# Heads in cycles of three steps, with the sums of own and of cross keys copied out of PSUM in two parts

## The chip, the cores and the metric

The kernel runs on one core of one Trainium2 chip. The metric is the device time of one execution in microseconds (us): the median of the runs shown. The profile is of one such execution.

## What is computed

One decoder layer with the norms after each part, for 8 sequences of 512 rows with 256 channels, and a context of 1024 rows with 128 channels each:

```python
x = layernorm(x + linear_attention(x))       # 16 heads of 64, relu features
x = layernorm(x + xattn(x, ctx))             # the part that the change touches
x = layernorm(x + top1_moe(x))               # 8 experts, 256 -> 1024 -> 256

# xattn: 16 heads of 16 channels
att  = causal(q @ k.T * scale)               # 512 x 512: own keys
y    = softmax(att) @ v
attc = qc @ kc.T * scale                     # 512 x 1024: cross keys
y    = y + softmax(attc) @ vc
out  = y @ Wp + bp
```

Each softmax has a sum of its own, so a head needs two sets of weighted values, one over own keys and one over cross keys, and each is divided by its own denominator.

## The kernel before

A loop over the 8 sequences (batches) computes both attentions and the routing, and after it a loop over tiles of rows runs the experts. The change is in the stretch of each batch that treats the 16 heads of the second attention, two at a time: 8 pairs (`PAIRS`). Head `a` of a pair lies in 64 of the 128 partitions, so the matmuls of the two heads use the two halves of TensorE's rows and can run side by side when they alternate.

The work of a pair is of these kinds. The names are those of the list `ORDER`, which every engine walks through in the same order and takes its own part of:

- **max** (22 for each pair, `MAXES`): TensorE computes scores of queries by keys for one head (L773 for cross keys, one matmul of 512 columns; L770 for own keys), into one of three PSUM banks, and VectorE reduces the bank to the row maxima (L1412; L1408 for own keys, with the causal mask). The banks are a ring of `MBANKS = 3`: an entry of the ring waits in `ring_slot` until the entry three places earlier has been read.
- **row**: when all maxima of a pair are there (VectorE's small `mpad` operation, L1419), TensorE turns them around (L781) into a bank of the same ring, and ScalarE copies them to `mrow` (L1193, four copies).
- **exp** (11 steps for each pair, `NU`: 3 for own keys, 8 for cross keys): TensorE computes the scores again, keys by queries, for both heads, and subtracts the maxima with a second matmul (L807 and L809 for cross keys, L800 and L803 for own keys). ScalarE takes the exponential (L1201) from PSUM into one of four buffers in SBUF (`ERING = 4`). There are two PSUM places for the scores, so the scores of step k wait until the exponential of step k-2 is through: `pe.wait_ge(s_exp, cur(b, NEXP, k - 1))`. The exponential of step k waits until step k-4 has been weighed. For own keys, GpSimd cuts the upper triangle off (L661).
- **weigh** (11 for each pair): TensorE multiplies values by exponentials (L837) and sums them in one PSUM bank, `zbank`: its left half for own keys, its right half for cross keys. Four such matmuls use four groups of 32 columns of the array at once. Each stands as 8 records of 256 columns where a step is of cross keys.
- **keep**: ScalarE copies `zbank` to `zk` (L1210). **turn**: TensorE turns `zk` around (L848) into a bank of the ring, ScalarE copies it out (L1218), VectorE takes the reciprocals (L1425), and GpSimd does the divisions and the addition.
- **part**: pieces of other matmuls (the query features of the next batch, L857), at the start and at the end of the stretch.

`heads_order` writes the list by hand. In the steady part it goes on by two steps at a time. With m for a max and E for an exp, one block is

```
[turn]  weigh weigh  m  E  m m  E  m
```

where the weighs are those of four and three steps before (`BEHIND = 4`). A row stands 4 or 6 maxima behind the last max of its pair (`ROW_AFTER`), in practice at the end of a block. If the last weigh of a pair has just been issued, and its keep with it, the first weigh of the next pair is put off to the end of the block (`late`), because it writes the bank that the keep reads. The maxima run ahead of the exps, so the last 15 steps of a batch have no max beside them.

On the way in, the maxima of the first pair and some of the second are mixed with `FIRST_PARTS`. On SyncE's queue, `free_slot` waits until a pair's last scores are computed before it loads the keys and queries of the pair five places on into its place.

Of the kernel before, what the change touches and what calls it, by code (L numbers as in the profile page):

```python
# [33 lines left out]
E, HID = 8, 1024  # L34
# [46 lines left out]
HB = 2  # L81
PAIRS = XH // HB
# [12 lines left out]
NSELF = len(EXP_SELF)  # L95
NU = NSELF + NTC
# [3 lines left out]
MAXES = NMU * HB  # L100
ERING = 4
AHEAD = 8
ROW_AFTER = (4, 6)
BEHIND = 4
LATER = 2

# [4 lines left out]
def head_half(j, a):  # L111
# [5 lines left out]
FIRST_PARTS = [("v", 1, 3), ("qc1", 0, 3), ("q1", 0, 3), ("k1", 0, 3),  # L117
               ("qf0", 0, 4), ("qf0", 1, 4), ("qf1", 0, 4), ("qf1", 1, 4)]
# [3 lines left out]
def heads_order():  # L122


    maxima = []
    for p in range(PAIRS):
        maxima += [("max", p, m) for m in range(MAXES)]
    for p in range(PAIRS):
        at = maxima.index(("max", p, MAXES - 1)) + 1 + (ROW_AFTER[p % 2] if p + 1 < PAIRS else 0)
        maxima.insert(at, ("row", p, 0))  # L130

    def take(count):
        taken = []
        while maxima and (count or maxima[0][0] == "row"):
            count -= maxima[0][0] == "max"
            taken.append(maxima.pop(0))
        return taken

    order = []
    for name, part, count in FIRST_PARTS:  # L140
        order += take(count)
        order.append(("part", name, part))
    order += take(MAXES + AHEAD - sum(count for _, _, count in FIRST_PARTS))
    turns, late = [], []
    steps = PAIRS * NU
    for k in range(0, steps + BEHIND, 2):
        weighed = late + [m for m in (k - BEHIND, k - BEHIND + 1) if m >= 0]
        late = []
        if turns:
            order.append(turns.pop())  # L150
        for m in weighed:
            if m % NU == 0 and m and order[-1] == ("keep", m // NU - 1, 0):
                late.append(m)
                continue
            order.append(("weigh", *divmod(m, NU)))
            if m % NU == NU - 1:
                order.append(("keep", m // NU, 0))
                turns.append(("turn", m // NU, 0))
        order += take(1)
        if k < steps:  # L160
            order.append(("exp", *divmod(k, NU)))
        order += take(HB)
        if k + 1 < steps:
            order.append(("exp", *divmod(k + 1, NU)))
        order += take(1)
        order += [("weigh", *divmod(m, NU)) for m in late]
        late = []
    assert not maxima
    return order + [("part", "qf2", 0)] + turns + [("part", "qf2", 1)]


ORDER = heads_order()


# [17 lines left out]
NEXP = PAIRS * NU  # L192


TILE = 128
TH = TILE // P
NTILE = (B * T + E * (TILE - 1)) // TILE
assert NTILE % 2 == 1
MORE = T // TILE
CR = C + 1  # L200
E_STEPS = 30
NOBODY = float(1 << 20)
# [28 lines left out]
def attentions(nc, x, xT, ctxT, wqkT, wv_l, rf, w_out, b_out, wk, bk, wq, bq, wv, bv, wck, bck,  # L231
# [9 lines left out]
    with ctx:  # L241
        def sb(name, shape, dt=F32):
            return ctx.enter_context(nc.sbuf_tensor(name, shape, dt))
# [84 lines left out]
        zk = sb("zk", [P, 2, T // 2])  # L328
# [12 lines left out]
        iota = sb("iota", [P, B * NT])  # L341
        number = sb("number", [P, B * NT])
        upto = sb("upto", [P, NTILE])
        full_at = sb("full_at", [P, MORE])
        below = sb("below", [P, E + 1, E])
        ranked = sb("ranked", [P, (NT + 1) * E])
        place = sb("place", [P, E])
        room = sb("room", [P, E])
        over = sb("over", [P, E])
        more = sb("more", [P, E, MORE])  # L350
        fresh = sb("fresh", [P, E])
        prior = sb("prior", [P, E + 1, E])
        first = sb("first", [P, E + 1])
# [14 lines left out]
        zbank = ps[1][:, BANK:2 * BANK]  # L368
# [33 lines left out]
        s_av = sem("s_av")  # L402
# [4 lines left out]
        s_keep = sem("s_keep")  # L407
# [15 lines left out]
        def cur(b, per, k):  # L423

            return b * per + (per + k)
# [269 lines left out]
        def _(pe):  # L695
# [116 lines left out]
            def weigh(b, p, n):  # L812


                if p == 0 and n == 0:
                    pe.wait_ge(s_vone, b + 1)
                if n == 0:
                    pe.wait_ge(s_keep, cur(b, PAIRS, p))
                e, own = es[:, (p * NU + n) % ERING], n < NSELF
                if own:  # L820
                    pe.wait_ge(s_cut, cur(b, PAIRS * NSELF, p * NSELF + n + 1))
                else:
                    pe.wait_ge(s_exp, cur(b, NEXP, p * NU + n + 1))
                z = zbank[:, 0:T // 2] if own else zbank[:, T // 2:T]
                for j, col in (EXP_SELF[n] if own else [(n - NSELF, 0)]):
                    first = j if own else 0
                    for f in range(2):
                        tiles = [t for t in (f, f + 2) if t >= first]
                        if not tiles:
                            continue  # L830
                        for a in range(HB):
                            at = a * BANK + col + (tiles[0] - first) * P
                            weights = e[:, at:at + P] if len(tiles) == 1 else \
                                e[:, a * BANK + col:a * BANK + col + T].rearrange("p (c f t) -> p c f t", c=2, f=2)[:, :, f, :] \
                                if first == 0 else e[:, at:at + 3 * P].rearrange("p (c t) -> p c t", c=3)[:, 0:3:2, :]
                            row = (f * HB + a) * ZW
                            last = mm(z[row:row + VW, (2 - len(tiles)) * P:2 * P], (va if own else vca)[:, j, p * HB + a, :], weights,  # L837
                                      start=n in (0, NSELF), stop=n in (NSELF - 1, NU - 1))
                last.then_inc(s_av, 1)

            def turn_results(b, p):

                pb = ring_slot(b, ("turn", p, 0))
                pe.wait_ge(s_keep, cur(b, PAIRS, p + 1))
                for w in range(2):
                    for c in range(2):
                        col = (w * 2 + c) * P
                        last = tr(pb[:, col:col + P], zk[:, w, c * P:(c + 1) * P], ident[:])  # L848
                last.then_inc(s_ring, 1)
# [37 lines left out]
            with pe.Fori(0, nb) as b:  # L887
# [17 lines left out]
                t = ready(b, "g0")  # L905
# [11 lines left out]
                t = ready(b, "g1")  # L917
# [197 lines left out]
        def _(act):  # L1115
            act.sem_inc(s_mrow, PAIRS)
            act.sem_inc(s_exp, NEXP)
            act.sem_inc(s_keep, PAIRS)
            act.sem_inc(s_zt, PAIRS - 1)

            def relu_q(i, t):
# [10 lines left out]
            with act.Fori(0, nb) as b:  # L1132
# [69 lines left out]
                                         eslot[k % 2][:].rearrange("p (a c) -> p a c", a=HB)[:, :, 0:w],  # L1202
                                         ACT.Exp, scale=SCALE).then_inc(s_exp, 1)

                def keep(p):

                    act.wait_ge(s_av, cur(b, NEXP, (p + 1) * NU))
                    if p:
                        act.wait_ge(s_ring, cur(b, NRING, RING_AT["turn", p - 1, 0] + 1))
                    nc.scalar.activation(zk[:].rearrange("p w t -> p (w t)"), zbank, ACT.Copy).then_inc(s_keep, 1)  # L1210

                def turned(p):

# [6 lines left out]
                for kind, p, n in ORDER:  # L1220
                    if kind == "row":
                        maxima_rows(p)
                    elif kind == "turn" and p < PAIRS - 1:
                        turned(p)
                    elif kind == "exp":
                        exp_unit(p, n)
                    elif kind == "keep":
                        keep(p)
                    elif p == "v":
                        values()  # L1230
                    elif p == "qc1":
                        act.wait_ge(s_nearc, (b + 1) * NEARC)
                        whole_part("qc1", 3)
                    elif p == "q1":
                        act.wait_ge(s_near, (b + 1) * NEAR)
                        whole_part("q1", 2)
                    elif p == "k1":
                        whole_part("k1", 0)
                    elif kind == "part" and n == 1:
                        relu_q(int(p[-1]), full(p)).then_inc(s_act, 1)  # L1240
# [14 lines left out]
        def _(dve):  # L1255
# [37 lines left out]
            v.tensor_copy(tri[:], y_s[:, 0, 0:P])  # L1293
            v.tensor_copy(upto[:, 0:B * NT], iota[:])
            v.tensor_scalar(upto[:, B * NT:NTILE], iota[:, 0:NTILE - B * NT], float(B * NT), None, ALU.add)
            v.tensor_scalar(full_at[:], iota[:, 0:MORE], float(TILE), None, ALU.mult)
            v.tensor_tensor(below[:], iota[:, 0:E + 1].unsqueeze(2).broadcast_to([P, E + 1, E]),
                            iota[:, 0:E].unsqueeze(1).broadcast_to([P, E + 1, E]), ALU.is_gt)
            v.reduce_sum(minus_f[:], ident[:].rearrange("p (b c) -> p c b", c=MROW)[:, 0:2, :], AX.X)
# [24 lines left out]
            with dve.Fori(0, nb) as b:  # L1324
                def step(ins):

                    steps[0] += 1
                    ins.then_inc(s_dstep, 1)
                    dve.wait_ge(s_dstep, b * NSTEP + steps[0])
# [141 lines left out]
                def by_tile(of):  # L1471
                    return of[:].unsqueeze(1).broadcast_to([P, NT, E])

                step(v.tensor_tensor(over[:], total, room[:], ALU.subtract))
                step(v.tensor_tensor(more[:], over[:].unsqueeze(2).broadcast_to([P, E, MORE]),
                                     full_at[:].unsqueeze(1).broadcast_to([P, E, MORE]), ALU.is_gt))
                step(v.reduce_sum(fresh[:], more[:], AX.X))
                step(v.tensor_tensor(prior[:], below[:], fresh[:].unsqueeze(1).broadcast_to([P, E + 1, E]), ALU.mult))
                step(v.reduce_sum(first[:], prior[:], AX.X))
# [346 lines left out]
```

## Time and profile before

| | |
|---|---|
| Median of 3 runs | 2287.46 us (2287.35 to 2288.9) |
| The profiled execution | 2287.69 us, of which the span from first to last instruction is 2286.0 us |
| TensorE busy | 2169.5 us (95%) |
| VectorE busy | 1366.7 us (60%) |
| ScalarE busy | 1102.2 us (48%) |
| GpSimd busy | 367.5 us (16%) |
| Mean granted TensorE clock | 0.994 of full speed |

Busy is the time in which at least one instruction of the engine was running. Matmuls are pipelined and their ends are modelled, so TensorE reads as busy in much of the time in which it does not start anything. Starts are more telling: the time from the start of one group of matmuls to the start of the next is what the group cost. In a line of the timeline, xN is the number of instructions of one kind that were merged, and the second number is the time from the start of the first to the end of the last. The time in brackets is how long the engine sat idle before, and who released it.

### The profile page before, as it was taken

To read this page: it belongs to the slowest core of one execution; us is meant where nothing else is said; L and a number is where in the kernel's file an instruction comes from. 1 tells how busy PE (TensorE), PEld (TensorE's weight loads), DVE (VectorE), ACT (ScalarE), POOL (GpSimd) and SP (SyncE) were. 2 spreads that over 40 slices of the span, in tenths; PEclk is the share of its full clock that TensorE was granted. 3 is DMA by queue.
4 is the path that set the end of the run, shared out by engine and by line. 5 is a ranking of instruction groups with operands and counts; after the bars stand their busy time and mean duration, and the time that the engine had idled before them with its cause. 6 is when DMAs were issued, how large, how long until landed. Compare 5 with 4: busy or idle time off the path is not lost. (4 is left out here: it accounts for less than half of the span.)

```text
span 2286.0 us, 51067 instructions
## 1 busy us (share of the span) xinstructions
PE 2169.5 (95%) x16290; PEld 1352.2 (59%) x16291; DVE 1366.7 (60%) x3905; ACT 1102.2 (48%) x1680; POOL 367.5 (16%) x628
## 2 busy tenths in 40 slices
PE   8999999999899999999999999999999899799998
PEld 4555554556455555555555645554555455499997
DVE  2588357844785458635883478357844685255554
ACT  1267524761477227732674257524762377233332
POOL 1011111111111111111111111111111111122222
PEclk9999999999999999999999999999999999899999
DMA  7440025102520162005300350026102520655553
GB/s 235 155 164 25 2 106 200 48 2 85 198 71 2 47 234 73 2 11 189 130 25 9 141 180 25 1 97 209 48 2 85 198 71 2 221 181 182 183 182 109
DMA packets 115763, 235.75 MB, mean 103 GB/s; under 512 B 19614, under 2 KB 42655, under 8 KB 113344
## 3 DMA queue, kind: packets, MB, share of 16 engines
q1 hardware_dynamic: 112112, 224.23, 29.3%
q0 software_dynamic: 3408, 8.41, 1.0%
q8 instruction: 137, 2.24, 0.4%
q14 instruction: 106, 0.87, 0.1%
HBM read 154.04 MB, written 73.17 MB: 99 GB/s over the span
## 5 line engine op out<-in xcount | busy, mean ns | idle before, releaser
L1201 ACT ACTIVATE es<-ps 128x1024 f32<-128x1024 f32 (+1 forms) x704 | 665.3, 984 | 250.7 <-PE ps L809 181.4
L1412 DVE TENSOR_REDUCE craw<-ps 128x1 f32<-128x512 f32 x1024 | 636.7, 684 | 115.0 <-PE ps L773 115.0
L773 PE MATMUL ps<-hk,hq 64*128 64x512 f32 x1024 | 391.4, 450 | 24.7 <-DVE craw L1412 8.6
L807 PE MATMUL ps<-hq,hk 64*128 64x512 f32 x1024 | 325.0, 440 | 2.2 <-ACT es L1201 2.2
L1408 DVE CUSTOM_DVE_ANT_0 ps<-ps,causal 128x512 f32<-128x512 f32 (+3 forms) x512 | 236.2, 518 | 91.4 <-PE ps L770 91.0
L773 PEld LDWEIGHTS ps<-hk,hq 64*128 64x128 f32 x1024 | 174.7, 184 | 194.8 <-DVE craw L1412 129.3
L809 PE MATMUL ps<-mrow,minus 64*128 64x512 f32 x1024 | 285.8, 391 | 0.0
L837 PE MATMUL ps<-es,vca 128*17 128x256 f32 x4096 | 276.6, 382 | 1.2 <-ACT es L1201 0.3
L661 POOL TENSOR_SCALAR_AFFINE_SELECT es<-es 128x256 f32<-128x256 f32 x256 | 99.0, 406 | 659.5 <-ACT es L1201 659.4
L1731 ACT ACTIVATE hT<-ph,b1s 128x128 f32<-128x128 f32 x312 | 89.2, 369 | 182.8 <-PE ph L1694 182.8
L809 PEld LDWEIGHTS ps<-mrow,minus 64*128 64x128 f32 x1024 | 166.0, 186 | 10.1
L807 PEld LDWEIGHTS ps<-hq,hk 64*128 64x128 f32 x1024 | 141.4, 184 | 32.0 <-ACT es L1201 20.8
L837 PEld LDWEIGHTS ps<-es,vca 128*17 128x17 f32 x4096 | 93.9, 97 | 109.9 <-issue 39.1
L770 PE MATMUL ps<-hk,hq 64*128 64x512 f32 (+3 forms) x512 | 142.8, 351 | 6.7 <-DVE craw L1408 6.2
L1694 PEld LDWEIGHTS ph<-xinT,w1s 128*128 128x128 f32 x1248 | 147.2, 194 | 3.0 <-issue 1.1
L1694 PE MATMUL ph<-xinT,w1s 128*128 128x128 f32 x1248 | 147.6, 277 | 0.7 <-ACT xinT L1721 0.7
L857 PE MATMUL ps<-xT_s,wqf 128*128 128x512 f32 x288 | 138.5, 607 | 5.0 <-ACT whole L1178 3.3
L1707 PE MATMUL py<-w2s,hT 128*128 x624 | 141.2, 380 | 0.0
L867 PE MATMUL ps<-wkf,xT_s 128*128 128x512 f32 x288 | 130.4, 597 | 0.0
L800 PE MATMUL ps<-hq,hk 64*128 64x512 f32 (+3 forms) x512 | 125.0, 337 | 4.3 <-ACT big_a L1122 4.3
L770 PEld LDWEIGHTS ps<-hk,hq 64*128 64x128 f32 x512 | 82.8, 184 | 74.7 <-DVE craw L1408 32.0
L1707 PEld LDWEIGHTS py<-w2s,hT 128*128 128x128 f32 x624 | 115.7, 190 | 13.9
(210 smaller groups left out, 2838.3 us busy)
## 6 DMA issues: line engine op xcount, KB each, us to landing
w1s<-in_w1T SPq DMA_DIRECT2D x39, 1024.0 KB, 5.4
hk<-scr_kc SPq DMA_DIRECT2D x64, 512.0 KB, 5.1
scr_kc<-staged SPq DMA_DIRECT2D x16, 1024.0 KB, 4.3
scr_qc<-staged SPq DMA_DIRECT2D x32, 512.0 KB, 4.5
scr_q<-staged SPq DMA_DIRECT2D x32, 512.0 KB, 5.3
hq<-scr_qc SPq DMA_DIRECT2D x56, 256.0 KB, 4.4
hq<-scr_q SPq DMA_DIRECT2D x56, 256.0 KB, 4.2
hk<-scr_k SPq DMA_DIRECT2D x56, 256.0 KB, 4.6
```

The lines of the kernel that those rows point to most:

```text
L770: last = mm(pb[:, col:col + w], hq[i][at, t * P:(t + 1) * P], hk[i][at, 0:w], start=True, stop=True)
L773: last = mm(pb, hq[i][at, T + t * P:T + (t + 1) * P], hk[i][at, T + half * BANK:T + (half + 1) * BANK], start=True, stop=True)
L807: mm(pb[a], hk[i][rows[a], T + j * P:T + (j + 1) * P], hq[i][rows[a], T:2 * T], start=True, stop=False)
L809: last = mm(pb[a], neg[a], mrow[p % 2][rows[a], :], start=False, stop=True)
L837: last = mm(z[row:row + VW, (2 - len(tiles)) * P:2 * P], (va if own else vca)[:, j, p * HB + a, :], weights, start=n in (0, NSELF), stop=n ...
L857: last = mm(t[:, a * T:(a + 1) * T], wqf[:, c, j * P:(j + 1) * P], xT_s[:, c, :], start=c == 0, stop=c == KC - 1)
L867: last = mm(t[:, half * 512:(half + 1) * 512], xT_s[:, c, i * P:(i + 1) * P], wkf[:, c, half * 512:(half + 1) * 512], start=c == 0, stop=c ...
L1201: nc.scalar.activation(es[:, k % ERING, :].rearrange("p (a c) -> p a c", a=HB)[:, :, 0:w], eslot[k % 2][:].rearrange("p (a c) -> p a c", a ...
L1408: last = v.tensor_tensor_reduce(own, own, causal[:, (NT - 1 - t) * P:NT * P], 1.0, LOWEST, ALU.add, ALU.max, craw[p % 2][:, t, a:a + 1, 0])
L1412: last = v.reduce_max(craw[p % 2][:, t, a:a + 1, 1 + half], pb, AX.X)
L1694: last = mm(ph[g % 2][:, a * TILE:(a + 1) * TILE], w1s[i][:, k, (GROUP * c + a) * P:(GROUP * c + a + 1) * P], xinT[i][:, k, :], start=k == ...
L1707: last = mm(py[i][:, n, 0:C], hT[i][:, c, n * P:(n + 1) * P], w2s[:, bass.ds(e * (NHC * C) + c * C, C)], start=c == 0, stop=c == NHC - 1)
```

## The change

`heads_order` is written anew. In the steady part it goes on by three steps at a time (`CYCLE = 3`). One cycle is

```
[turn]  weigh weigh weigh  [keep]  m  E  m m  E  m m  E  m  [row]
```

with the weighs of steps k-4, k-3 and k-2 ahead of the exps of steps k, k+1 and k+2. A batch has 31 such cycles where it had 46 blocks (the last two of each list with less in them). The first two cycles have two maxima more at their end (`MORE = 2`, `MORE_CYCLES = 2`), so the maxima end earlier: beside step 5 of the seventh pair, and not beside step 6. A row stands where a cycle ends. A turn stands at the start of the cycle after the one whose weighs end a pair.

A keep is now two: the left half of `zbank` is copied after the pair's third weigh, the right half after its eleventh, both at the end of the weighs of their cycle. No weigh is put off any more. TensorE waits for `s_keep` where a keep stands between a weigh and the one before it. The old constant `MORE` of the routing is renamed `MORE_TILES`. The core of the diff:

```diff
-ROW_AFTER = (4, 6)
+ROW_AFTER = 4
+MORE, MORE_CYCLES = 2, 2
+CYCLE = 3
...
+    def row_if_due(behind):
+
+        p = rows[0] if rows else None
+        if rows and (PAIRS - p - 1) * MAXES - behind >= len(maxima):
+            order.append(("row", rows.pop(0), 0))
...
     steps = PAIRS * NU
-    for k in range(0, steps + BEHIND, 2):
-        weighed = late + [m for m in (k - BEHIND, k - BEHIND + 1) if m >= 0]
-        late = []
+    for k in range(0, steps + BEHIND, CYCLE):
         if turns:
             order.append(turns.pop())
-        for m in weighed:
-            if m % NU == 0 and m and order[-1] == ("keep", m // NU - 1, 0):
-                late.append(m)
-                continue
+        for m in range(max(0, k - BEHIND), min(steps, k - BEHIND + CYCLE)):
             order.append(("weigh", *divmod(m, NU)))
-            if m % NU == NU - 1:
-                order.append(("keep", m // NU, 0))
+            if m % NU == NSELF - 1:
+                kept.append(("keep", m // NU, 0))
+            elif m % NU == NU - 1:
+                kept.append(("keep", m // NU, 1))
                 turns.append(("turn", m // NU, 0))
-        order += take(1)
-        if k < steps:
-            order.append(("exp", *divmod(k, NU)))
-        order += take(HB)
-        if k + 1 < steps:
-            order.append(("exp", *divmod(k + 1, NU)))
-        order += take(1)
-        order += [("weigh", *divmod(m, NU)) for m in late]
-        late = []
+        order.extend(kept)
+        kept = []
+        take(1)
+        for n in range(k, min(steps, k + CYCLE)):
+            order.append(("exp", *divmod(n, NU)))
+            take(HB if n + 1 < k + CYCLE else 1 + (MORE if k < MORE_CYCLES * CYCLE else 0))
+        row_if_due(min(ROW_AFTER, len(maxima)) if maxima else 0)
...
-                if n == 0:
-                    pe.wait_ge(s_keep, cur(b, PAIRS, p))
+                if n == 0 or KEPT_AT[p, n] > KEPT_AT[p, n - 1]:
+                    pe.wait_ge(s_keep, cur(b, 2 * PAIRS, KEPT_AT[p, n]))
...
-                def keep(p):
-
-                    act.wait_ge(s_av, cur(b, NEXP, (p + 1) * NU))
-                    if p:
+                def keep(p, w):
+
+                    act.wait_ge(s_av, cur(b, NEXP, KEEP_AFTER[p, w]))
+                    if p and w == 0:
                         act.wait_ge(s_ring, cur(b, NRING, RING_AT["turn", p - 1, 0] + 1))
-                    nc.scalar.activation(zk[:].rearrange("p w t -> p (w t)"), zbank, ACT.Copy).then_inc(s_keep, 1)
+                    nc.scalar.activation(zk[:, w, :], zbank[:, w * (T // 2):(w + 1) * (T // 2)], ACT.Copy).then_inc(s_keep, 1)
```

## Rows read from the trace of the kernel before

**Rows 1.** The page's first line.
```profile
span 2286.0 us, 51067 instructions
```

**Rows 2.** Busy time of each engine from a batch's opening to the end of its heads.
```profile
1092.52:1222.79 130.27, 125.83 (x1319) 73.16 (x1318) 93.51 (x232) 97.11 (x131) 19.93 (x46) 1.00 0.14 48
```

**Rows 3.** Line L1210 in the whole span: minimum, median, maximum in ns, first and last.
```profile
L1210 ACT ACTIVATE zk<-ps x64: 597/603/606, 149.7 to 1945.4; 128x512 f32<-128x512 f32 x64
```

**Rows 4.** Timeline of PE in the steady part, start and length in us.
```profile
1137.95 0.49 PE L773 MATMUL ps<-hk,hq 64*128 64x512 f32 x1
...
1139.22 0.50 PE L773 MATMUL ps<-hk,hq 64*128 64x512 f32 x1
1139.90 0.32 PE L781 MATMUL ps<-ident,mpad 128*128 128x128 f32 x1 [0.17 <-DVE craw L1412]
1140.15 1.06 PE L837 MATMUL ps<-es,vca 128*17 128x256 f32 x16
...
1142.94 1.06 PE L837 MATMUL ps<-es,vca 128*17 128x256 f32 x16
...
1145.63 0.41 PE L837 MATMUL ps<-es,vca 128*17 128x256 f32 x4
```

**Rows 5.** Timeline of DVE in the same stretch.
```profile
1138.48 2.48 DVE L1412 TENSOR_REDUCE craw<-ps 128x1 f32<-128x512 f32 x4 [0.28 <-PE ps L773]
```

**Rows 6.** Timeline of ACT in the same stretch.
```profile
1138.94 1.94 ACT L1201 ACTIVATE es<-ps 128x1024 f32<-128x1024 f32 x2 [0.95 <-PE ps L809]
```

**Rows 7.** Timeline of PE at a batch's opening, before its first weigh.
```profile
1095.71 0.49 PE L800 MATMUL ps<-hq,hk 64*128 64x256 f32 x2
...
1096.19 1.09 PE L773 MATMUL ps<-hk,hq 64*128 64x512 f32 x2
1096.87 0.64 PE L807 MATMUL ps<-hq,hk 64*128 64x512 f32 x2
...
1097.44 0.44 PE L773 MATMUL ps<-hk,hq 64*128 64x512 f32 x1
1097.81 1.28 PE L837 MATMUL ps<-es,va 128*17 128x256 f32 x20
```

**Rows 8.** Timeline of DVE in the opening and just after it.
```profile
1093.05 6.07 DVE L1412 TENSOR_REDUCE craw<-ps 128x1 f32<-128x512 f32 x10 [1.64 <-PE ps L773]
...
1102.88 0.46 DVE L1408 CUSTOM_DVE_ANT_0 ps<-ps,causal 128x256 f32<-128x256 f32 x1
...
1103.63 1.29 DVE L1412 TENSOR_REDUCE craw<-ps 128x1 f32<-128x512 f32 x2
```

**Rows 9.** Timeline of ACT in the opening.
```profile
1094.63 2.43 ACT L1201 ACTIVATE es<-ps 128x1024 f32<-128x1024 f32 x3 [0.98 <-PE ps L803]
1097.86 1.02 ACT L1201 ACTIVATE es<-ps 128x1024 f32<-128x1024 f32 x1 [0.80 <-PE ps L809]
```

**Rows 10.** Line L1425 among the groups of two pairs, busy us and mean ns.
```profile
L1425 DVE RECIPROCAL rec<-zt 128x16 f32<-128x16 f32 x4 | 1.0, 249 | 0.0
```

**Rows 11.** Timeline of PE where no maxima are left.
```profile
1203.78 0.50 PE L807 MATMUL ps<-hq,hk 64*128 64x512 f32 x2
...
1204.45 1.06 PE L837 MATMUL ps<-es,vca 128*17 128x256 f32 x16
1205.44 0.50 PE L807 MATMUL ps<-hq,hk 64*128 64x512 f32 x2
...
1206.67 1.06 PE L837 MATMUL ps<-es,vca 128*17 128x256 f32 x16
...
1212.90 0.63 PE L837 MATMUL ps<-es,va 128*17 128x256 f32 x8
1213.46 0.66 PE L848 MATMUL ps<-ident,zk 128*128 128x128 f32 x4
1214.05 1.06 PE L837 MATMUL ps<-es,va 128*17 128x128 f32 x20
```

**Rows 12.** Timeline of ACT in the same stretch.
```profile
1206.22 1.94 ACT L1201 ACTIVATE es<-ps 128x1024 f32<-128x1024 f32 x2 [0.27 <-PE ps L809]
```

More of the change, by code:

```diff
@@ L122, in heads_order @@
 def heads_order():
[L125 to L130, printed above, removed]
-    def take(count):
[L133 to L137, printed above, removed]
@@ L139, in heads_order @@
-    order = []
+    maxima = [("max", p, m) for p in range(PAIRS) for m in range(MAXES)]
+    order, rows, turns, kept = [], list(range(PAIRS)), [], []
+    def take(count):
+        order.extend(maxima[:count])
+        del maxima[:count]
+    def row_if_due(behind):
+        p = rows[0] if rows else None
+        if rows and (PAIRS - p - 1) * MAXES - behind >= len(maxima):
+            order.append(("row", rows.pop(0), 0))
     for name, part, count in FIRST_PARTS:
-        order += take(count)
+        take(count)
+        row_if_due(ROW_AFTER)
@@ L142, in heads_order @@
         order.append(("part", name, part))
-    order += take(MAXES + AHEAD - sum(count for _, _, count in FIRST_PARTS))
-    turns, late = [], []
+    take(MAXES + AHEAD - sum(count for _, _, count in FIRST_PARTS))
     steps = PAIRS * NU
-    for k in range(0, steps + BEHIND, 2):
-        weighed = late + [m for m in (k - BEHIND, k - BEHIND + 1) if m >= 0]
-        late = []
+    for k in range(0, steps + BEHIND, CYCLE):
         if turns:
             order.append(turns.pop())
-        for m in weighed:
-            if m % NU == 0 and m and order[-1] == ("keep", m // NU - 1, 0):
-                late.append(m)
-                continue
+        for m in range(max(0, k - BEHIND), min(steps, k - BEHIND + CYCLE)):
@@ L192 @@
 NEXP = PAIRS * NU
+KEPT_AT = {(p, n): sum(f[0] == "keep" for f in ORDER[:i]) for i, (kind, p, n) in enumerate(ORDER) if kind == "weigh"}
+KEEP_AFTER = {(p, n): sum(f[0] == "weigh" for f in ORDER[:i]) for i, (kind, p, n) in enumerate(ORDER) if kind == "keep"}
 TILE = 128
@@ L198 @@
 assert NTILE % 2 == 1
-MORE = T // TILE
+MORE_TILES = T // TILE
 CR = C + 1
@@ L343, in attentions @@
         upto = sb("upto", [P, NTILE])
-        full_at = sb("full_at", [P, MORE])
+        full_at = sb("full_at", [P, MORE_TILES])
         below = sb("below", [P, E + 1, E])
@@ L349, in attentions @@
         over = sb("over", [P, E])
-        more = sb("more", [P, E, MORE])
+        more = sb("more", [P, E, MORE_TILES])
         fresh = sb("fresh", [P, E])
@@ L843, in turn_results @@
                 pb = ring_slot(b, ("turn", p, 0))
-                pe.wait_ge(s_keep, cur(b, PAIRS, p + 1))
+                pe.wait_ge(s_keep, cur(b, 2 * PAIRS, 2 * p + 2))
                 for w in range(2):
@@ L1117, in _ @@
             act.sem_inc(s_exp, NEXP)
-            act.sem_inc(s_keep, PAIRS)
+            act.sem_inc(s_keep, 2 * PAIRS)
             act.sem_inc(s_zt, PAIRS - 1)
@@ L1227, in _ @@
                     elif kind == "keep":
-                        keep(p)
+                        keep(p, n)
                     elif p == "v":
@@ L1295, in _ @@
             v.tensor_scalar(upto[:, B * NT:NTILE], iota[:, 0:NTILE - B * NT], float(B * NT), None, ALU.add)
-            v.tensor_scalar(full_at[:], iota[:, 0:MORE], float(TILE), None, ALU.mult)
+            v.tensor_scalar(full_at[:], iota[:, 0:MORE_TILES], float(TILE), None, ALU.mult)
             v.tensor_tensor(below[:], iota[:, 0:E + 1].unsqueeze(2).broadcast_to([P, E + 1, E]),
@@ L1474, in _ @@
                 step(v.tensor_tensor(over[:], total, room[:], ALU.subtract))
-                step(v.tensor_tensor(more[:], over[:].unsqueeze(2).broadcast_to([P, E, MORE]),
-                                     full_at[:].unsqueeze(1).broadcast_to([P, E, MORE]), ALU.is_gt))
+                step(v.tensor_tensor(more[:], over[:].unsqueeze(2).broadcast_to([P, E, MORE_TILES]),
+                                     full_at[:].unsqueeze(1).broadcast_to([P, E, MORE_TILES]), ALU.is_gt))
                 step(v.reduce_sum(fresh[:], more[:], AX.X))
```

## The prediction

> **What bounds the kernel now.** I read the page first, for the span [rows 1], then the busy time of each engine over the heads of one batch [rows 2]. The reader is to see that no engine alone explains the 130.27 us: TensorE reads as busy for 125.83, but its matmuls are pipelined, VectorE works 93.51 and ScalarE 97.11. The heads are 8 times 130.27 = 1042 us, 46% of the span: of the 64 keeps, 8 in a batch, the first stands at 149.7 and the last at 1945.4 [rows 3], which is 7 periods of about 241 us and one batch's own stretch between. The experts behind them are untouched.
>
> Then I read timelines of starts, to find what paces a block. Four rules come out, and the rest is made of them.
>
> *VectorE's beat.* Ten reductions in a row take 6.07 us, start to end, so one starts every 0.60 [rows 8], and four take 2.48 [rows 5]; I use 0.61. Six are 3.66.
>
> *The ring gate.* A max's matmul starts at 1137.95 and its reduction at 1138.48: 0.53 later. The fourth max of that block starts at 1139.22, which is 0.74 after the start of the reduction (0.68 long) that frees its bank. The row waits for the second reduction, which started 0.61 behind the first, at 1139.09, and starts at 1139.90: 0.81 [rows 4, 5].
>
> *ScalarE's gate.* In the opening, the exponential of the first step starts at 1094.63 [rows 9]. One takes 1.02 [rows 9], so it ends at 1095.65, and the scores of the third step start at 1095.71 [rows 7]: 0.06 later. In a block, the exponential starts 0.99 behind the block's first matmul (1137.95 to 1138.94 [rows 4, 6]).
>
> *Phases of TensorE.* A group of two weighs of cross keys holds TensorE from 1204.45 to 1205.44, 0.99, and a single one from 1212.90 to 1213.46, 0.56 [rows 11]. So a weigh adds 0.43, and three take 1.42. A whole block that nothing holds up takes 1145.63 - 1142.94 = 2.69 [rows 4]: 0.99 of weighs and 1.70 of scores. In it the fourth max may start 0.53 + 0.74 = 1.27 behind the first by the ring gate, just when it comes up in the order anyway. The block of two steps is as long as three banks allow, and VectorE needs 2.44 of its 2.69.
>
> **The change, part by part.**
>
> *Fewer and longer groups of weighs.* In a batch they go from 47 to 30. Without gates a cycle would cost TensorE 1.42 of weighs and 18 matmuls of scores instead of 12. Three more pairs of them, one pair every 0.23 (two steps of eight matmuls hold 1205.44 to 1206.67, 1.23, one step 1203.78 to 1204.45, 0.67 [rows 11], the difference with one new start in it being 0.56 for two pairs; inside a step a pair follows in 0.23), bring 1.70 to 2.38. That is 3.80 for three steps where three are now 1.5 x 2.69 = 4.04.
>
> *The ring gate in a cycle.* A cycle has six maxima between two groups of weighs. The banks are still three, so the sixth needs the third reduction: it can't start before 0.53 + 2 x 0.61 + 0.74 = 2.49 behind the first. The fifth can't before 1.88, and the third step's scores stand behind it.
>
> *ScalarE's gate in a cycle.* The third step's scores use the place of the first step's: 0.99 + 1.02 + 0.06 = 2.07. From their start to the weighs it takes what the opening shows for the same order (scores, one max, weighs): 1096.87 to 1097.81, 0.94 [rows 7]. So the weighs start at 3.01, and the cycle is 1.42 + 3.00 = 4.42 us. By the ring gate alone it is 2.49 + 0.37 (1097.44 to 1097.81) + 1.42 = 4.28. I take 4.42, since both gates hold. Three steps cost 0.4 us more than three free ones of before. VectorE shows why: during the weighs it has the last three banks and no more, 1.8 us of work, then it stands still for over 0.5 until the next max arrives. Ten cycles of a batch are of this plain kind: 44.2.
>
> *Rows.* A row behind the sixth max needs the bank of the fourth: the reduction of that starts at 0.53 + 3 x 0.61 = 2.36, and the row can start 0.81 later, 3.17, and holds TensorE 0.25 (1139.90 to 1140.15 [rows 4]): 1.42 + 3.42 = 4.84. Where the reciprocal, 0.25 [rows 10], comes first on VectorE, as in most of them, it is 5.1. With one of them behind a shorter group of weighs (the own keys' third step) six such cycles are 29.9.
>
> *Turns.* A turn stands behind a cycle's last max and before its weighs, so it needs the bank of two reductions before: 3.12, and 0.59 for itself (1213.46 to 1214.05 [rows 11]): 5.1 with plain maxima. Where the own keys' maxima are ahead of it, VectorE is slower (from the last own reduction to the next one 0.75 with the `mpad` operation, 1102.88 to 1103.63 [rows 8], where plain ones follow in 0.61), and the weigh of the second step must wait for two cuts. I get 5.5 and 5.9 for those, 27.2 for the five.
>
> *The opening* is 5.29 up to the first weigh (1092.52 [rows 2] to 1097.81 [rows 7]), at VectorE's beat, and stays. The cycle after it has eight maxima, 5.4, and the last one with maxima holds a row and a turn behind the `mpad`, 6.3.
>
> *The tail.* It has 16 steps after these and no maxima, so only ScalarE's gate counts. The exponential starts 0.78 behind the scores (1205.44 to 1206.22 [rows 11, 12]), the third step's scores at 0.78 + 1.02 + 0.06 = 1.86, the weighs 0.67 on, at 2.53: a cycle of 3.95. Now two steps take 1206.67 - 1204.45 = 2.22 [rows 11], three 3.33. Five cycles of 3.95 less 0.2 for a shorter first group, one turn (0.6) and 3.8 for the last exponentials and weighs come to 24.0.
>
> *Keeps.* Eight more copies a batch. Two halves cost between 0.60 (the whole, [rows 3]) and 1.20 (each as long as it), so 0 to 0.6 more for a pair; I take nothing, because ScalarE works 97 of 130 us and the copies fall between the start of the scores and the exponential 0.99 behind it. Without that cover a batch would pay up to 5 us. The new waits on `s_keep` come a whole cycle behind the copy. Queued behind them are the weighs and then the maxima, but they don't bite. The weigh that was put off no longer is: a start of a group, 0.13 each, is in the counts.
>
> *Queues.* SyncE's `free_slot` waits for scores of a pair five places back, and its loads are used about two pairs later; no DMA is added or gets into the way. GpSimd has the same work.
>
> **The sum** for a batch: 5.29 + 5.4 + 44.2 + 29.9 + 27.2 + 6.3 + 24.0 = 142.3 us, against 130.27 now [rows 2]: +12.0. For eight batches +96. The profiled execution took 2287.69 for a span of 2286.0 [rows 1], 0.2 above the median. So 2383 us.
>
> One rule of the Trainium skill speaks for the change. *TensorEngine Tiling (Array Packing)*, Key Properties, says that going from one tiling mode to another drains TensorE, and scores (64-row tiles) and weighs (32-column tiles) are two modes. By that, the trace agrees: the last max of the opening starts 0.37 before the weighs [rows 7], where pairs within a mode follow in 0.23. [...] The same page's PSUM Bottleneck says that tiling doesn't speed up what empties PSUM, and this is the side on which I forecast.
>
> **The rivals.**
>
> *TensorE decides* (0.08). The gates are softer than I read them, and only the borders count: 3.80 for 4.04, 0.24 x 29 = 7 us a batch, 2232. It needs a reduction of 0.35 us or less, since the sixth max would have to start at 1.96 = 0.53 + 2d + 0.74. Against it: 0.61, and the opening, where ten maxima in a row run at just that beat.
>
> *It evens out* (0.04). Blocks of now aren't all free: 46 of them and the turns take 130, and 1.5 free blocks would do for less. If these hold-ups were gone in longer cycles, a change within 0.2% is possible.
>
> *Borders absorb rows and turns* (0.16). They cost now on top of free blocks; in a cycle held up anyway they might hide, and the tail might keep its present pace. Then 11 cycles cost 4.5 and not 5.2, and the tail 4 us less: about +4 a batch, 2320.
>
> *More than that* (0.04). Own reductions and `mpad` hold cycles up that I counted as plain; 0.4 for each pair would be +26, 2409.
>
> **How the numbers follow.** My forecast has 0.68: 2383, own range 2345 to 2400. The lower end is all plain cycles at 4.28, turns and rows at their shortest and half the tail's loss, +58. The upper end is the part of `mpad` left out. The 8-in-10 range reaches down into the absorbed case and a little into the last one: 2318 to 2403. About 0.2% (5 us) is what a measurement can tell from nothing. Faster 0.08, same 0.04, slower 0.88.
>
> **What would show it.** The heads of a batch take about 142 us, with 30 groups of weighs, 24 records and 1.42 us each. In a plain cycle the reductions come in one run of six, 3.66 long, with VectorE idle for 0.5 to 0.7 before the first. The sixth max starts 2.5 to 2.7 behind the first. In the waits, TensorE's for L1412 goes up, and a wait for ScalarE's L1201 appears on L807. In the tail, the weighs start every 3.95 us. It is wrong if weighs follow each other in 3.8, or if the third step's scores start before the first exponential ends.

## The result and the profile after

The changed kernel takes 2379.68 us (median of 4 runs, 2379.22 to 2382.45), the kernel before 2287.4 (4 runs): a ratio of 1.0407, 95% interval 1.039 to 1.0423. The forecast was 2383 us.

The page of the changed kernel begins like this (busy us, share of the span, instructions):

```profile
span 2377.6 us, 51267 instructions
## 1 busy us (share of the span) xinstructions
PE 2211.1 (93%) x16290; PEld 1388.5 (58%) x16291; DVE 1366.4 (57%) x3905; ACT 1113.2 (47%) x1744; POOL 366.4 (15%) x628
```

VectorE and ScalarE do what they did, within 1%, in 91.6 us more. So it is waiting. The busy time of each engine over one batch, from the first max behind `qf1` to the end of the heads, answers to [rows 2]:

```profile
1137.34:1279.12 141.78, 131.14 (x1319) 77.59 (x1318) 93.51 (x232) 98.71 (x139) 19.86 (x46) 1.00 0.13 44
```

141.78 us against 130.27 is 11.5 more for a batch and 92 for eight: all of the difference lies here. VectorE's 93.51 us are the same to the last digit.

A plain cycle is where one is to look. TensorE's timeline, from its first max at 1188.58 to the next cycle's at 1192.97, answers to [rows 4]:

```profile
1188.58 0.50 PE L772 MATMUL ps<-hk,hq 64*128 64x512 f32 x1
...
1189.86 1.09 PE L772 MATMUL ps<-hk,hq 64*128 64x512 f32 x2
1190.65 0.54 PE L806 MATMUL ps<-hq,hk 64*128 64x512 f32 x2
1190.99 0.43 PE L808 MATMUL ps<-mrow,minus 64*128 64x512 f32 x2
1191.22 0.39 PE L772 MATMUL ps<-hk,hq 64*128 64x512 f32 x1
1191.55 1.49 PE L836 MATMUL ps<-es,vca 128*17 128x256 f32 x24
1192.97 0.50 PE L772 MATMUL ps<-hk,hq 64*128 64x512 f32 x1
```

VectorE's timeline of the same stretch, which answers to [rows 5]:

```profile
1185.55 2.42 DVE L1411 TENSOR_REDUCE craw<-ps 128x1 f32<-128x512 f32 x4
1189.11 3.68 DVE L1411 TENSOR_REDUCE craw<-ps 128x1 f32<-128x512 f32 x6 [1.15 <-PE ps L772]
1193.51 2.48 DVE L1411 TENSOR_REDUCE craw<-ps 128x1 f32<-128x512 f32 x4 [0.71 <-PE ps L772]
```

And ScalarE's, which answers to [rows 6]:

```profile
1189.57 2.91 ACT L1200 ACTIVATE es<-ps 128x1024 f32<-128x1024 f32 x3 [0.99 <-PE ps L808]
```

The cycle takes 4.39 us. Its six reductions are one run of 3.68, and then VectorE stands for 0.71 until the next cycle's first max. The third step's scores start at 1190.65, 2.07 into the cycle: the first exponential ends at 1189.57 + 1.02 = 1190.59. The pair of maxima at 1189.86 stretches over 1.09 us because the second of them waited for its bank; it started 1.09 less its own 0.50 behind 1189.86, at about 1190.45. The weighs of three steps take 1.42 (1191.55 to 1192.97).

The list of waits (us in total, times, longest) shows where TensorE and its weight loads (PEld) waited. For ScalarE's exponentials they waited longer: the second of these lines was 20.8 in the kernel before and the third 2.2. The first, the wait for VectorE's reductions of cross keys, was 129.3 then and hardly moved, so it says nothing for or against the ring gate:

```profile
PEld ps L772 <- DVE craw L1411: 126.6, 272, 1.0
...
PEld ps L806 <- ACT es L1200: 49.8, 80, 1.1
...
PE ps L806 <- ACT es L1200: 22.3, 32, 0.8
```

Where no maxima are left, TensorE's timeline answers to [rows 11]:

```profile
1271.37 1.49 PE L836 MATMUL ps<-es,vca 128*17 128x256 f32 x24
1272.79 0.50 PE L806 MATMUL ps<-hq,hk 64*128 64x512 f32 x2
...
1274.63 0.50 PE L806 MATMUL ps<-hq,hk 64*128 64x512 f32 x2 [0.66 <-ACT es L1200]
...
1275.29 1.49 PE L836 MATMUL ps<-es,vca 128*17 128x256 f32 x24
```

The weighs start every 3.92 us, and in a plain cycle TensorE stands for about 0.66 until the first exponential is through. The blocks of two steps took 2.22.

### The profile page after: what moved, and what is told of

It is laid out like the page before. It is cut to its first block and busy times, and to the rows that moved or that the text cites. A ratio compares the mean times of both kernels' runs of the same rounds, so it can differ in the third digit from the quotient of the medians.

```text
span 2377.6 us, 51267 instructions
## 1 busy us (share of the span) xinstructions
PE 2211.1 (93%) x16290; PEld 1388.5 (58%) x16291; DVE 1366.4 (57%) x3905; ACT 1113.2 (47%) x1744; POOL 366.4 (15%) x628
## 5 line engine op out<-in xcount | busy, mean ns | idle before, releaser
L1200 ACT ACTIVATE es<-ps 128x1024 f32<-128x1024 f32 (+1 forms) x704 | 657.6, 984 | 227.0 <-PE ps L808 179.8
L772 PE MATMUL ps<-hk,hq 64*128 64x512 f32 x1024 | 405.5, 453 | 36.2 <-DVE craw L1407 10.2
L806 PE MATMUL ps<-hq,hk 64*128 64x512 f32 x1024 | 304.0, 440 | 23.4 <-ACT es L1200 22.3
L836 PE MATMUL ps<-es,vca 128*17 128x256 f32 x4096 | 270.0, 382 | 4.5 <-ACT es L1200 4.5
L808 PE MATMUL ps<-mrow,minus 64*128 64x512 f32 x1024 | 266.7, 391 | 0.0
L806 PEld LDWEIGHTS ps<-hq,hk 64*128 64x128 f32 x1024 | 135.1, 184 | 60.0 <-ACT es L1200 49.8
L836 PEld LDWEIGHTS ps<-es,vca 128*17 128x17 f32 x4096 | 104.5, 97 | 109.9 <-ACT es L1200 27.0
L808 PEld LDWEIGHTS ps<-mrow,minus 64*128 64x128 f32 x1024 | 149.0, 186 | 10.7
L856 PE MATMUL ps<-xT_s,wqf 128*128 128x512 f32 x288 | 137.7, 605 | 4.8 <-ACT whole L1177 3.2
L799 PE MATMUL ps<-hq,hk 64*128 64x512 f32 (+3 forms) x512 | 118.2, 338 | 9.4 <-ACT es L1200 5.2
```

What stands on the lines that cost most here:

```text
L772: last = mm(pb, hq[i][at, T + t * P:T + (t + 1) * P], hk[i][at, T + half * BANK:T + (half + 1) * BANK], start=True, stop=True)
L806: mm(pb[a], hk[i][rows[a], T + j * P:T + (j + 1) * P], hq[i][rows[a], T:2 * T], start=True, stop=False)
L808: last = mm(pb[a], neg[a], mrow[p % 2][rows[a], :], start=False, stop=True)
L856: last = mm(t[:, a * T:(a + 1) * T], wqf[:, c, j * P:(j + 1) * P], xT_s[:, c, :], start=c == 0, stop=c == KC - 1)
L1200: nc.scalar.activation(es[:, k % ERING, :].rearrange("p (a c) -> p a c", a=HB)[:, :, 0:w], eslot[k % 2][:].rearrange("p (a c) -> p a c", a ...
```

## The experiments

Twelve kernels ran on the chip; their ratios are to the kernel before, timed beside them. Six of them leave out part of the maxima or of the exponentials, only to shorten VectorE's or ScalarE's work.

**The change without its longer cycle** (called c2 below).

```diff
-MORE, MORE_CYCLES = 2, 2
-CYCLE = 3
+MORE, MORE_CYCLES = 0, 2
+CYCLE = 2
```

> The changed kernel with CYCLE = 2 and MORE = 0, so blocks of two steps, four maxima and two weighs as before, but still two keeps for each pair, the waits on the halves and no weigh put off. Theory (the length of the cycle costs, through the ring of three banks and the two places for scores): the heads of a batch are back at about 130 us and the time at 2283 to 2290 us. Rival (the keeps in two parts and the waits on them cost): the time stays above 2320 us.

Measured: 2277.69 us, ratio 0.9957 (0.9943 to 0.9971), a little below the range. The length of the cycle and the extra maxima are the whole loss: 2379.7 - 2277.7 = 102 us, more than the change lost in all. What is left of the change (two keeps, rows at a block's end, no weigh put off) gains 10 us. The steady part is as long as before (104.2 us from the first weigh to the last max, it was 104.1); the tail is 19.35 us and was 20.54. In the kernel before, the last pair's row doesn't stand at the end of a block but between the scores of steps 6 and 7 of the seventh pair, just ahead of [rows 11]; it waited 1.29 us for VectorE's `mpad` with nothing else to do:

```profile
1203.53 0.33 PE L781 MATMUL ps<-ident,mpad 128*128 128x128 f32 x1 [1.29 <-DVE mpad L1419]
```

In this kernel the row stands at the block's end and waited less:

```profile
1196.32 0.40 PE L806 MATMUL ps<-hq,hk 64*128 64x512 f32 x2
1196.55 0.40 PE L808 MATMUL ps<-mrow,minus 64*128 64x512 f32 x2
1197.79 0.33 PE L780 MATMUL ps<-ident,mpad 128*128 128x128 f32 x1 [0.84 <-DVE mpad L1418]
1198.05 1.06 PE L836 MATMUL ps<-es,vca 128*17 128x256 f32 x16
```

The block with that row takes 3.18 us and took 3.85. The rest of the 1.2 us, some 0.5, is the turn of the seventh pair, where no weigh is put off any more: two blocks' parts of 2.05 and 1.14 became one of 2.70.

**Cycles of three steps only while there are maxima.** `heads_order` takes two steps at a time once the list of maxima is empty:

```diff
+        cycle = CYCLE if maxima else TAIL
...
-        for n in range(k, min(steps, k + CYCLE)):
+        for n in range(k, min(steps, k + cycle)):
```

> The changed kernel with cycles of three steps as long as there are maxima, and blocks of two steps after that. Theory: in the tail the third step's scores wait for the first step's exponential, a cycle of 3.95 us where three steps in blocks of two take 3.33, so five such cycles give back about 3 us a batch, 25 us in all: 2355 us. Rival (the tail is limited by ScalarE either way and its share of the loss is nothing): 2380 us.

Measured: 2348.55 us, ratio 1.0275 (1.0258 to 1.0292), 31 us less than the changed kernel. From the last max to the last weigh a batch takes 22.1 us, not 26.2. The theory holds and the size was 6 us too small. Of the 4.1 us a batch, five cycles of 3.95 where three steps took 3.33 are 3.1. I had the 3.33 from one block of 2.22; the plain blocks of the tail here take 2.07 to 2.30, 2.17 in the mean. The rest isn't divided up further.

**Both kernels with shorter reductions and exponentials.**

```diff
-    last = v.reduce_max(craw[p % 2][:, t, a:a + 1, 1 + half], pb, AX.X)
+    last = v.reduce_max(craw[p % 2][:, t, a:a + 1, 1 + half], pb[:, 0:256], AX.X)
...
-    w, k = E_COLS[n], p * NU + n
+    w, k = E_COLS[n] if p * NU + n < 2 * ERING else min(256, E_COLS[n]), p * NU + n
```

> The changed kernel with the reduction of each bank of cross keys cut to 256 of its 512 columns, and the exponentials from the ninth step of a batch on cut to 256 of 512 columns for each head: part of the maxima and of the exponentials isn't computed. Theory: a reduction then starts every 0.35 us and an exponential takes 0.6, both gates open, and a plain cycle falls from 4.39 to 3.8 us, cycles with rows and turns fall by somewhat more, the tail's to about 3.5: 18 us a batch, about 2236 us. Rival (the two keeps, or TensorE's order of work itself, cost): the time falls no more than that of the kernel before does with the same cuts.

> The kernel before with the same two cuts (part of the maxima and exponentials isn't computed). Theory: its blocks of two steps are hardly held up, 2.69 us stays 2.69, only rows, turns and own keys' maxima gain, some 5 us a batch: about 2247 us, and now the cycles of three steps are the faster by about 10 us. Rival: the kernel before stays faster than the changed one by about 90 us.

Measured: the changed kernel 2281.95 us (ratio 0.9978, 0.9969 to 0.9988), the kernel before 2222.45 (0.9718, 0.9699 to 0.9738). The lead of the kernel before fell from 92 to 60 us, but it didn't turn round. This expectation failed, and the trace says by what. TensorE's timeline of a plain cycle of the changed kernel:

```profile
1154.34 1.49 PE L836 MATMUL ps<-es,vca 128*17 128x256 f32 x24
1155.76 0.49 PE L772 MATMUL ps<-hk,hq 64*128 64x512 f32 x1
...
1157.41 0.60 PE L799 MATMUL ps<-hq,hk 64*128 64x512 f32 x2
...
1158.30 0.41 PE L836 MATMUL ps<-es,vca 128*17 128x256 f32 x4
```

And ScalarE's timeline of the same cycle:

```profile
1156.76 1.29 ACT L1200 ACTIVATE es<-ps 128x512 f32<-128x512 f32 x2 [1.07 <-PE ps L808]
```

An exponential of 0.60 from 1156.76 ends at 1157.36, and the third step's scores start at 1157.41: the gate still holds, at 1.65. The cycle is 3.96 and not 3.8. And the plain block of the kernel before wasn't free, as I had it, but fell from 2.69 to 2.58 us where all its steps are of cross keys.

**The two cuts one by one**, in the changed kernel: the first edit of the diff above alone, and the second alone.

> The changed kernel with only the reductions of cross keys cut to 256 of 512 columns (part of the maxima isn't computed). Theory (two gates hold at nearly one place): the ring gate opens, but the third step's scores still wait for the first exponential, 2.07 us into the cycle, so a plain cycle stays at 4.3 to 4.4 us; only cycles with a row or a turn gain, 3 to 5 us a batch: about 2345 us. Rival (the ring gate alone is the cause): plain cycles fall to 3.8 us, 15 us a batch, about 2260 us.

> The changed kernel with only the exponentials from the ninth step on cut to 256 of 512 columns (part of them isn't computed). Theory: the scores' gate opens, the ring gate stays, a plain cycle falls only from 4.39 to 4.28 us, the tail's from 3.95 to 3.5: about 3.5 us a batch, 2350 us. Rival (ScalarE's gate alone is the cause): plain cycles fall to 3.8 us and the time to about 2260 us.

Measured: 2354.93 us with short reductions (ratio 1.0295, 1.0278 to 1.0312), 2353.43 with short exponentials (1.0284, 1.0267 to 1.0301). Both gates are there, one behind the other. With short reductions, a plain cycle, from 1141.39 to 1145.78, takes 4.39 us as before:

```profile
1141.39 0.50 PE L772 MATMUL ps<-hk,hq 64*128 64x512 f32 x1
...
1143.47 0.50 PE L799 MATMUL ps<-hq,hk 64*128 64x512 f32 x2
...
1145.78 0.50 PE L772 MATMUL ps<-hk,hq 64*128 64x512 f32 x1
```

The third step's scores are at 2.08. With short exponentials it takes 4.32, from 1142.44 to 1146.76, and the scores come at 1.96, behind the fifth max:

```profile
1142.44 0.50 PE L772 MATMUL ps<-hk,hq 64*128 64x512 f32 x1
...
1143.72 1.10 PE L772 MATMUL ps<-hk,hq 64*128 64x512 f32 x2
1144.40 0.64 PE L799 MATMUL ps<-hq,hk 64*128 64x512 f32 x2
...
1146.76 0.49 PE L772 MATMUL ps<-hk,hq 64*128 64x512 f32 x1
```

Each alone gains 25 or 26 us (2345 and 2350 us were expected), the two together 98. In the plain cycle each alone gives 0 and 0.07 us, the two together 0.43. Of the 26 us of the short exponentials most is in the tail, where there is only ScalarE's gate: from the last max to the last weigh it takes 23.6 us and not 26.2, 21 us for eight batches. Neither rival, that one gate alone is the cause, holds.

**Both kernels with the gates open.** As above with 128 columns, and the reductions of own keys cut to 128 columns for each tile too.

```diff
-    own = pb[:, col:col + (t + 1) * P]
-    last = v.tensor_tensor_reduce(own, own, causal[:, (NT - 1 - t) * P:NT * P], 1.0, LOWEST,
+    own = pb[:, col:col + P]
+    last = v.tensor_tensor_reduce(own, own, causal[:, (NT - 1) * P:NT * P], 1.0, LOWEST,
...
-    last = v.reduce_max(craw[p % 2][:, t, a:a + 1, 1 + half], pb, AX.X)
+    last = v.reduce_max(craw[p % 2][:, t, a:a + 1, 1 + half], pb[:, 0:128], AX.X)
...
-    w, k = E_COLS[n], p * NU + n
+    w, k = E_COLS[n] if p * NU + n < 2 * ERING else min(128, E_COLS[n]), p * NU + n
```

> The changed kernel with reductions of 128 columns for each bank or tile of own keys, and exponentials of 128 columns for each head from the ninth step on (most of the maxima and exponentials isn't computed). With 256 columns a plain cycle still showed both gates: the fifth max waited for the second reduction, and the third step's scores for the first exponential (1.65 us into the cycle). Theory: with 0.35 us or so for an exponential and less than 0.3 for a reduction both gates open, a plain cycle takes 3.6 to 3.7 us, the own keys' cycles lose most, and the lead of the blocks of two, 60 us with 256 columns, shrinks to 15 or turns round. Rival (something else in the order of three steps costs, the turns, the keeps or the third weigh): the lead stays at 40 us or more.

> The kernel before with the same cuts to 128 columns. Theory: its plain blocks stay at about 2.58 us, as with 256 columns, three steps in 3.87; rows and own keys gain a little: about 2210 us, and the changed one within 15 us of it. Rival: this one is faster than the changed one by 40 us or more.

Measured: the changed kernel 2195.74 us (ratio 0.9599, 0.9583 to 0.9615), the kernel before 2185.01 (0.9555, 0.9539 to 0.9571). The lead of the kernel before is 11 us of the 92. The plain cycle of the changed one is 3.78 us, and its timeline shows no wait:

```profile
1132.36 1.49 PE L836 MATMUL ps<-es,vca 128*17 128x256 f32 x24
1133.78 0.49 PE L772 MATMUL ps<-hk,hq 64*128 64x512 f32 x1
...
1135.28 0.47 PE L806 MATMUL ps<-hq,hk 64*128 64x512 f32 x1
...
1136.14 0.41 PE L836 MATMUL ps<-es,vca 128*17 128x256 f32 x4
```

A plain block of the kernel before, all of cross keys, takes 2.58 us:

```profile
1065.81 1.06 PE L837 MATMUL ps<-es,vca 128*17 128x256 f32 x16
...
1068.38 0.84 PE L837 MATMUL ps<-es,vca 128*17 128x256 f32 x12
```

So three steps in blocks of two take 1.5 x 2.58 = 3.87 there, and the plain cycle of three steps has no cost of its own. From the first max of the stretch to the start of the last weigh, a batch takes 120.0 us in the changed kernel and 118.4 in the kernel before; without the cuts it is 141.5 and 129.9. So 10.0 of the 11.6 us that a batch lost hang on how long VectorE and ScalarE take: they are the two gates and, in the opening, the extra maxima at VectorE's beat. Part of the 1.6 us that are left is in the tail, where even an exponential of 0.38 is waited for: three steps take 3.30 there, and 1.5 x 2.12 = 3.18 in blocks of two. The rest lies where maxima still run. Cycles with a turn still take 4.4 to 5.4 us here, and in one of them TensorE waits 0.39 us for VectorE's reductions of own keys, so for those cycles the gate wasn't quite open.

**Rows and turns behind the weighs.** In `heads_order`, the turn and the row that is due are put in after a group of weighs and not before it, once in c2 and once in the changed kernel. The order of the ring's entries is the same.

```diff
-        if turns:
-            order.append(turns.pop())
+        turned = turns.pop() if turns else None
...
+        row_if_due(min(ROW_AFTER, len(maxima)) if maxima else 0)
+        if turned:
+            order.append(turned)
         order.extend(kept)
...
-        row_if_due(min(ROW_AFTER, len(maxima)) if maxima else 0)
```

> The kernel of c2 with the rows and the turns moved from before a block's weighs to behind them; the order of the ring is the same. Theory: a row or a turn waits for the ring's bank (0.25 us for a row, 0.2 for a turn, above what it takes itself), and behind the weighs the bank has long been read, so about 0.25 x 7 + 0.2 x 6 = 3 us a batch go: 2260 to 2268 us, faster than the kernel before. Rival (the wait only moves to the next block, since VectorE gets its next bank later by the length of the row or turn): no more than 5 us off c2.

> The changed kernel with the rows and turns moved behind the weighs in the same way. Theory: in cycles of three the wait of a row or a turn is about 0.4 us, 13 of them, 4 to 5 us a batch: about 2343 us, still slower than the kernel before. Rival (as for c2_moved): 2375 us or more.

Measured: 2273.38 us in blocks of two (ratio 0.9936, 0.9919 to 0.9953), 4 us off c2, so the rival's number holds and the theory's doesn't. A wait moves to the next block: a block and the next one with a row behind its weighs take 2.69 + 3.52 = 6.21 us, and took 3.19 + 2.79 = 5.98 with the row before them; with a turn it is 2.69 + 3.51 = 6.20, and was 3.52 + 2.91 = 6.43. What the turns gained the rows gave back: from the first weigh to the last max a batch takes 104.3 us and took 104.2. Most of the 4 us is from the tail, 18.95 us and not 19.35. In cycles of three it is 2362.25 (1.0323, 1.0306 to 1.034), 17 us off the changed kernel and half of what the theory gave; neither theory nor rival has the number right. The intervals of c2 and this one overlap, so which is the faster isn't settled; both are faster than the kernel before.

**No extra maxima at the start.**

```diff
-MORE, MORE_CYCLES = 2, 2
+MORE, MORE_CYCLES = 0, 2
```

> The changed kernel with MORE = 0: no two maxima more at the end of the first two cycles, so the maxima end two steps later. Theory: the first cycle after the opening falls from 5.7 to 4.7 us or less, for the eight maxima in it ran at VectorE's beat, but a plain cycle with maxima takes the place of a faster one of the tail, 0.3 to 0.5 us: 0.5 to 1 us a batch, 2372 to 2376 us. Rival (maxima that are ahead pay back later): 2385 us.

Measured: 2357.02 us, ratio 1.0306 (1.0289 to 1.0323), 23 us less than the changed kernel, where 4 to 8 were expected. The sign was right, the size a miss. I had forgotten that the cycle of steps 0 to 2 has two more maxima as well, and these stand before the batch's first weigh, at VectorE's beat. In the changed kernel, the first weigh starts 5.30 us behind the first max of the stretch:

```profile
1137.34 0.73 PE L772 MATMUL ps<-hk,hq 64*128 64x512 f32 x3
...
1142.64 1.28 PE L836 MATMUL ps<-es,va 128*17 128x256 f32 x20
```

Without `MORE` it starts 4.10 behind it:

```profile
1125.89 0.73 PE L772 MATMUL ps<-hk,hq 64*128 64x512 f32 x3
...
1129.99 0.63 PE L836 MATMUL ps<-es,va 128*17 128x256 f32 x8
```

From the first weigh to the last a batch takes 134.8 us and not 136.2: 1.2 + 1.4 = 2.6 a batch, 21 us.

**Neither extra maxima nor a tail in threes.** 

```diff
-MORE, MORE_CYCLES = 2, 2
+MORE, MORE_CYCLES = 0, 2
...
+        cycle = CYCLE if maxima else TAIL
```

> The changed kernel with both MORE = 0 and blocks of two steps once the maxima have ended, so that only the cycles with maxima are of three steps. It is the difference to c2 that counts: what the steady cycles of three steps cost by themselves. Theory: 23 us (MORE) and 31 us (tail) add up, the second a little less since the tail is two steps shorter: 2325 to 2332 us, and the 48 to 54 us that are left above c2 are the steady cycles. Rival (the parts overlap, and the tail's loss was largely the last cycle's row and turn): 2340 us or more.

Measured: 2333.94 us, ratio 1.0205 (1.0188 to 1.0222), 2 us above the theory's range. From the changed kernel to c2, 102 us, it is 23 us for the extra maxima, 23 more for the tail, and 56 for the cycles of three steps while there are maxima, of which a batch has 25 here. The shares depend on the order in which the parts are taken out: the tail alone gave 31 us, since with the extra maxima it is two steps longer.

## Why the prediction was right

*What bounds the kernel.* Right: the loss is in the heads, 11.5 us a batch for 12.0 predicted, with VectorE's work unchanged and ScalarE's 1.6 us more. Term by term, from weigh to weigh in one batch: the opening 5.29 us as forecast, the cycle after it 5.70 for 5.4, ten plain ones 44.0 for 44.2, six with a row 29.2 for 29.9, five with a turn 27.8 for 27.2, the last with maxima 6.0 for 6.3, the tail 23.9 for 24.0. No term is off by more than 0.7, and part of the errors cancel: that the sum is off by only 0.5 is a little luck.

*The ring gate and ScalarE's gate.* Right, and shown by experiments: the fifth max about 1.88 behind the first, the third step's scores at 2.07, a plain cycle of 4.39 us for 4.42. Short reductions alone leave it at 4.39, short exponentials alone at 4.32 (the ring alone was put at 4.28), and both with 128 columns bring 3.78. One sign named in the forecast didn't come: TensorE's waits for the reductions of cross keys were to go up and stayed at 127 us for 129. VectorE's idle time of 0.71 ahead of its six reductions, the sixth max at 2.64 and the waits for ScalarE did come.

*Rows and turns.* Right in the mean. Cycles with a row took 4.61 to 5.01 us for 4.84 to 5.1, those with a turn 5.26 to 5.75 for 5.1 to 5.9, and the one with both 6.0 for 6.3. In a cycle where the own keys' maxima are ahead of a turn, TensorE's timeline shows the wait for the bank behind VectorE's slower reductions: 0.77 from one max to the next, 0.39 of it as idle time:

```profile
1199.28 0.38 PE L769 MATMUL ps<-hk,hq 64*128 64x256 f32 x1
1200.05 0.50 PE L772 MATMUL ps<-hk,hq 64*128 64x512 f32 x1 [0.39 <-DVE craw L1407]
```

*The tail.* Right: 3.92 for 3.95, and blocks of two give 31 us back in it.

*The keeps.* The forecast of nothing fits, but no run has it alone: a half takes 384 ns where the whole took 603 [rows 3], so a pair pays 0.17 more on ScalarE. c2 has all of these keeps and also four groups of weighs fewer, and is faster than the kernel before.

*What TensorE would take by itself.* This step was wrong, though the sum doesn't hang on it. I called the block of 2.69 us free, because its fourth max came up just when its bank did. With reductions and exponentials cut, to 256 or to 128 columns, it is 2.58 (no run cut only the reductions there). So three steps unhindered are 3.87 in blocks of two and 3.78 in cycles of three, measured, and not 4.04 and 3.80: longer groups of weighs save 0.1 us for three steps, not 0.24. The first rival's 2232 us was too good; even with both gates open the order of three steps gains nothing. The rule of the Trainium skill (*TensorEngine Tiling (Array Packing)*, Key Properties: a change of tiling mode drains TensorE) is borne out in sign by these runs, with 0.1 us saved where two borders take the place of three.

*The opening.* Its 5.29 us came as forecast, and the first full cycle took 5.70 for 5.4. What I hadn't seen is the price of the extra maxima in both: without them the opening takes 4.10 us and the first full cycle 4.75, and the time falls by 23 us. The sum had this cost inside its terms, but not under its name.

## What to carry to other kernels

Before making a group of work longer, count how many of each buffer the other engines can hold while it lasts. Here three banks are 1.8 us of VectorE's work: enough for a pause of 0.99 us, but in a pause of 1.42, with the latencies of 0.53 and 0.74 us at its ends, the engine stands still for 0.7, and no saving of 0.1 us on TensorE pays that. Gates that lie close together hide one another, so opening one alone (25 or 26 us) says little about both (98 us). And a change can have a good half: the details that came with the longer cycle, without it, make a kernel that is 0.4% faster than the one before.

## What the runs showed of the hardware that was not expected

In one of the eight batches of the changed kernel the stretch from the first to the last weigh was 137.7 us instead of 136.2. The windows of it show a granted clock of 0.66 over 5 us, that is about 3.4 us at the lower of TensorE's two levels (1.2 GHz) and the rest at 2.4:

```profile
1395.00:1400.00 5.00, 4.47 (x42) 2.67 (x30) 4.42 (x17) 2.96 (x3) 0.00 (x0) 1.00 0.13 52
1400.00:1405.00 5.00, 4.89 (x39) 2.52 (x38) 3.21 (x8) 1.30 (x2) 0.00 (x0) 0.66 0.01 3
1405.00:1410.00 5.00, 4.88 (x45) 2.82 (x47) 3.85 (x7) 4.18 (x9) 0.00 (x0) 1.00 0.00 0
```

TensorE reads as busy for 4.47 us of the 5 before it, 4.89 of the 5 with it and 4.88 of the 5 after. The kernel before had no such dip in its heads. In the profiles of the kernels in cycles of three with the extra maxima there are sixteen in all: one in the changed kernel, four with short reductions alone, three with both cuts to 256 columns, two with short exponentials alone, three in each of those with blocks of two in the tail and with rows and turns moved, none with the cuts to 128 columns. Each makes its batch about 1.5 us longer. Read from windows of 2 us, every one of them begins 5.6 to 6.2 us behind a batch's first weigh, about where the cycle with eight maxima ends, which takes 5.7 us in the changed kernel. In the kernels without the extra maxima none fell between the first weigh and the last; c2 and the kernel made from it with rows and turns moved had one elsewhere. So a few us of the extra maxima's cost can be the clock, and so can a spread of that size between kernels of this kind; no run tried what sets it off, so that stays open.
